# Reordering the last two attention rounds of an attention and mixture-of-experts kernel, and issuing each round's last weighted sum one slot later

## The reference, cut to what matters

```python
x = layernorm(x + attn(x))
scores = sigmoid(x @ router.T)            # 16 experts in 4 groups
...                                       # best 2 groups by (score + bias), best 4 experts in them
routed = sum over the 4 of weight * down_e(silu(gate_e(x)) * up_e(x))
x = layernorm(x + routed + shared(x))     # shared: two experts that see every token
```

## Time and profile before

| | |
|---|---|
| median of 3 runs | 1218.46 us (1216.24 to 1221.86) |
| the profiled execution's own time | 1211.09 us |
| its span, first to last instruction | 1209.3 us |
| mean granted TensorE clock | 0.936 of full speed |

### The profile page before, as it was taken

One profiled execution on the slowest core, in us unless ns is written; L12 is line 12 of the kernel. 1 busy time (PEld: TensorE's weight loads), 2 busy tenths in 40 slices (PEclk: granted clock), 3 DMA queues, 4 the chain that ended last, 5 costly groups with the idle time before them and its releaser, 6 DMA issues.

```text
span 1209.3 us, 25555 instructions
## 1 busy us (share of the span) xinstructions
PE 999.3 (83%) x8693; PEld 585.4 (48%) x8693; DVE 854.5 (71%) x1907; ACT 627.6 (52%) x1449; POOL 495.0 (41%) x712
## 2 busy tenths in 40 slices
PE   7976999879887999998899778888998787956950
PEld 3533333334432455555565445454564456845740
DVE  6666888768885667779767886788677669765543
ACT  4413777667444565755456457554565563314430
POOL 7922121133138211321473743113626745673334
PEclk9987999999888899999999999999999999987985
DMA  5843267421113444233276743222565744877942
GB/s 177 272 136 110 61 208 262 149 59 46 49 56 111 88 98 91 63 71 76 88 163 131 159 119 93 57 67 82 133 145 133 216 115 135 197 180 180 251 155 74
DMA packets 221978, 152.85 MB, mean 126 GB/s; under 512 B 139936, under 2 KB 199072, under 8 KB 221856
## 3 DMA queue, kind: packets, MB, share of 16 engines
q1 hardware_dynamic: 207936, 114.50, 37.5%
q0 software_dynamic: 12288, 33.57, 9.1%
q10 hardware_dynamic: 1632, 3.15, 0.9%
HBM read 50.36 MB, written 73.40 MB: 102 GB/s over the span
## 4 chain that ended last, share of the span: by engine, by line
PE 47%; DVE 17%; POOL 14%; issue 8%; DMA 5%; ACT 4%; SPq 4%; DVEq 0%; POOLq 0%; ACTq 0%
PE bank L711 11%; PE bank L566 9%; PE bank L537 8%; PE bank L550 7%; POOL a_pool L1021 6%; DVE a_mx L1201 4%; POOL rows L1013 3%; PE bank L724 3%; DMA a_pool<-outs,e_slot 2%; POOL a_PT L971 2%; DVE e_R L1447 2%; PE bank L596 2%; ACT a_PT L1082 2%; SPq L799 2%; PE bank L540 1%
## 5 line engine op out<-in xcount | busy, mean ns | idle before, releaser
L1201 DVE TENSOR_REDUCE a_mx<-bank 128x1 f32<-128x512 f32 (+3 forms) x720 | 423.6, 619 | 196.7 <-PE bank L540 123.0
L1082 ACT ACTIVATE a_PT<-bank 128x512 f32<-128x512 f32 (+4 forms) x832 | 373.6, 497 | 219.5 <-PE bank L550 215.9
L550 PE MATMUL bank<-a_QS,a_KS 113*128 113x512 f16 (+4 forms) x832 | 275.1, 338 | 31.9 <-DVE a_mx L1201 25.1
L971 POOL TENSOR_SCALAR_AFFINE_SELECT a_PT<-a_PT 128x256 f32<-128x256 f32 (+1 forms) x288 | 111.9, 395 | 437.5 <-ACT a_PT L1082 436.9
L537 PE MATMUL bank<-a_KS,a_QS 112*128 112x512 f16 (+4 forms) x832 | 264.3, 339 | 25.1 <-DMA a_KS<-k_dram 12.7
L566 PE MATMUL bank<-a_PT,a_VG 128*17 128x512 f32 (+4 forms) x1664 | 185.9, 519 | 28.1 <-POOL a_PT L971 28.1
L1021 POOL DMA_INDIRECT a_pool<-outs,e_slot x128 | 124.7, 975 | 82.2 <-issue 33.7
L1013 POOL DMA_INDIRECT rows<-e_XR,e_slot x128 | 127.8, 999 | 66.5 <-issue 35.4
L537 PEld LDWEIGHTS bank<-a_KS,a_QS 112*128 112x128 f16 x832 | 81.2, 100 | 121.8 <-ACT a_PT L1082 48.5
L1147 ACT ACTIVATE e_tq<-bank 128x256 f32<-128x256 f32 x136 | 51.1, 383 | 154.4 <-PE bank L711 154.0
L550 PEld LDWEIGHTS bank<-a_QS,a_KS 113*128 113x128 f16 x832 | 82.4, 100 | 98.9 <-DVE a_mx L1201 41.7
(11 more groups left out here) (156 smaller groups left out, 1289.1 us busy)
## 6 DMA issues: line engine op xcount, KB each, us to landing
outs<-e_ys SPq DMA_DIRECT2D x104, 256.0 KB
rows<-a_pool SPq DMA_DIRECT2D x48, 256.0 KB, 3.2
q_dram<-p_qk SPq DMA_DIRECT2D x32, 128.0 KB, 2.6
k_dram<-p_qk SPq DMA_DIRECT2D x32, 128.0 KB, 2.5
v_dram<-p_vs SPq DMA_DIRECT2D x8, 512.0 KB, 4.5
a_QS<-q_dram SPq DMA_DIRECT2D x64, 64.0 KB
a_KS<-k_dram SPq DMA_DIRECT2D x64, 64.0 KB
a_VG<-v_dram SPq DMA_DIRECT2D x16, 256.0 KB, 4.6
```

The source lines that it names most:

```text
L550: pe.matmul(ps[:, 0:(qc + 1) * CH - q0], KS[p][0:MR + 1, kt // NT, h % 2, kt % NT * P:kt % NT * P + P], QS[p][0:MR + 1, qc, h, q0 - qc * C ...
L971: pool.affine_select(out=a, in_=a, compare_op=ALU.is_ge, fill=0.0, base=q0 - (kt * P - WIN), pattern=[[0, 2], [1, w]], channel_multiplier= ...
L1082: act.activation(PT[(G + i) % 2][:, h, 0:w], bank("ST", G, i, h)[:, 0:w], ACT.Exp)\
L1201: dve.tensor_reduce(mx[:, piece, t // NT, heads[0]:heads[0] + n, t % NT], bank("S", G, u)[:, 0:n * w].rearrange("p (h k) -> p h k", h=n), ...
```

## The change

`SEQ` is a new order of the slots: rounds 0 to 13 as before, then first half of 14, first half of 15, second half of 14, second half of 15. Everything that counted slots (semaphore values, the two buffers of exponentials) now goes by `SLOT_NO`, the place in `SEQ`, and by `HALF_NO`. PE issues `weighted` of the slot before in each slot, across the ends of rounds too, and only the very last one at once; `out_copy` of a second half stands one slot into the next round. `shares` replaces `share`: it is the same for rounds 0 to 13, and for the last two the maximum's units are spread so that round 15's are done before each of its halves begins. The planner gets the chunks' places from the places of `outT`.

What the new plan puts where: for round 15's first half `maxT` at 372 and its store at 374, with scoresT of slot 187 (h = 374) needing it; for its second half 397 and 399, for h = 400. The first load of group 2 is at 372, `load_rows` for its eleventh pair is at 398 and needs the `gu` at 399. The first four slots of round 14 have 5, 6, 4 and 4 units instead of 4, 3, 3 and 3, and the fifth none instead of 2. Chunk 6's chain: `ont` 392 and 393, `x1t` 404 and 406, `lg` 409, `place` 422 to 425, scatters 425 to 435. Chunk 7's: `ont` 419 and 420, `lg` 434, `pos` 441. The last `gu` of group 2 is at 446 (two shared `gu` of chunk 6 and one more of group 2 between `pos` and it), the scatters of group 4 from 445, the gathers of group 2 from 459, the last `combine` of group 2 at 483, the last `y` at 535. Two `y` move from before 416 to behind it, and behind 483 there are 20 `gu` and 24 `y` of routed pairs as there were behind 482 before, and two shared `gu` and one `ysh` besides.

```diff
@@ -43,6 +43,17 @@
 FIRST = 1 + max(i for i, (qc, kt, _) in enumerate(SLOTS) if qc == 0 or kt < CH // P)
 ATT = NR * NSL

+PHASES = [(G, tuple(range(NH2))) for G in range(NR - 2)] + [(G, (half,)) for half in range(NH2) for G in (NR - 2, NR - 1)]
+SEQ = [(G, i) for G, halves in PHASES for i, (qc, _, _) in enumerate(SLOTS) if qc in halves]
+SLOT_NO = {at: n for n, at in enumerate(SEQ)}
+HALF_NO = {at: n for n, at in enumerate((G, half) for G, halves in PHASES for half in halves)}
+MASKED_TO = [sum(i in MASKED for _, i in SEQ[:n]) for n in range(ATT)]
+
+
+def last_read(G, half):
+
+    return SLOT_NO[G, max(i for i, (qc, kt, _) in enumerate(SLOTS) if half in (qc, kt * P // CH))]
+
...
-def share(slot):
-
-    cols = [(qc + 1) * CH - q0 + FIXED for qc, _, q0 in SLOTS]
-    lo, hi = (NU * sum(cols[:n]) // sum(cols) for n in (slot, slot + 1))
-    return [((n - TAIL) % NU, n >= TAIL) for n in range(lo, hi)]
+def shares():
+
+
+
+
+    at, ends_ = {}, {}
+
+    def spread(units, slots):
+        cols = [(SLOTS[i][0] + 1) * CH - SLOTS[i][2] + FIXED for _, i in slots]
+        for n, slot_ in enumerate(slots):
+            lo, hi = (len(units) * sum(cols[:m]) // sum(cols) for m in (n, n + 1))
+            at[slot_] = at.get(slot_, []) + units[lo:hi]
+
+    for G in range(NR - 2):
+        spread([(G, u) for u in range(NU - TAIL, NU)] + [(G + 1, u) for u in range(NU - TAIL)],
+               [(G, i) for i in range(NSL)])
+        ends_[G, 1], ends_[G, FIRST - 1] = (G, 1), (G + 1, 0)
+    G = NR - 2
+    first, last = ([i for i, sl in enumerate(SLOTS) if sl[0] == qc] for qc in range(NH2))
+    spread([(G, u) for u in range(NU - TAIL, NU)] + [(G + 1, u) for u in range(SECOND)], [(G, i) for i in first[:-1]])
+    spread([(G + 1, u) for u in range(SECOND, NU)], [(G + 1, i) for i in first] + [(G, i) for i in last[:-2]])
+    ends_[G, 1], ends_[G, first[-2]], ends_[G, last[-3]] = (G, 1), (G + 1, 0), (G + 1, 1)
+    return at, ends_
+
+
+SHARES, MAX_ENDS = shares()
...
+    for slot_, (G, half) in MAX_ENDS.items():
+        at = 2 * SLOT_NO[slot_] + (2 if G == NR - 1 and not half else 1 if half and G < NR - 1 else 3)
+        pe[at] = ("maxT", G, half)
+        act[at + 1].append(("mT", G, half))
+        sp[at + 2].append(("put_max", G, half))
+    out_at = {}
     for G in range(NR):
-        s0 = 2 * NSL * G
-        for (g, half, at) in ((G, 1, s0 + 3), (G + 1, 0, s0 + 2 * FIRST + 1)):
-            if g < NR:
-                pe[at] = ("maxT", g, half)
-                act[at + 1].append(("mT", g, half))
-                sp[at + 2].append(("put_max", g, half))
-        for qc, at in ((0, s0 + 2 * (HALF[0] + 3) + 1), (1, s0 + 2 * NSL + 5 if G < NR - 1 else s0 + 2 * NSL + 1)):
+        for qc in range(NH2):
+            last_slot = SLOT_NO[G, HALF[qc]]
+            out_at[G, qc] = at = 2 * last_slot + (7 if last_slot < ATT - 1 else 3)
             pe[at] = ("outT", G, qc)
             dve[at + 1].append(("normal", G, qc))
         if G + 2 < NR:
-            sp[s0 + 2 * FIRST + 1].append(("stack", G + 2, 0))
-            sp[s0 + 2 * NSL].append(("stack", G + 2, 1))
+            for half in range(NH2):
+                sp[2 * last_read(G, half) + 3 - half].append(("stack", G + 2, half))
         if G + 1 < NR:
-            sp[s0 + 4].append(("load_v", G + 1))
+            sp[2 * SLOT_NO[G, 0] + 4].append(("load_v", G + 1))

     for n in range(NX):
         at = 2 * (n // 3 * NSL + 4 * (n % 3) + 1)
@@ -143,7 +177,7 @@
     for n in range(UNITS_B):

     def chain(c, o, gap):

@@ -172,13 +206,12 @@

     ready, routed = {}, {}
...
-            pool[e + 4 if not late else tail - 10].append(("add_bo", c))
-            ready[c], at = chain(c, e, 0 if c == NC - 2 else 1)
-        gap = 1 if late else 2
+            e = out_at[b * NG + NG - 1, c % NH2] + (2 if c % NH2 == 0 else 1)
+            sp[min(e - 1, tail - 14)].append(("load_res", c))
+            pool[min(e + 4, tail - 10)].append(("add_bo", c))
+            ready[c], at = chain(c, e, 1)
+        gap = 1 if g == NGR - 1 else 2
         for n in range(RPARTS):
             dve[at + 2 + gap * n].append(("route", g, n))
         q = put(("pos", g), at + gap * RPARTS + 2)
@@ -195,7 +228,7 @@
             c, tile = shared_place(g, n)
             wanted.append((ready[c] + tile * 5, g, n))
         lo = routed[g] + 5
-        hi = routed[g + 1] - 7 if g + 2 < NGR and g < B - 2 else tail if g == B - 2 else lo
...
         lo = routed[g] + 5
-        hi = routed[g + 1] - 7 if g + 2 < NGR and g < B - 2 else tail if g == B - 2 else lo
+        hi = max(lo, min(routed[g + 1] - 7, tail)) if g + 1 < NGR else lo
...
         at = max(last[g] + 6, w)
-        if g == B - 2:
-            at = max(at, routed[NGR - 1] + 1)
         for t in range(GROUPS[g][2]):
...
             def weighted(G, i):
                 p = G % 2
                 qc, kt, q0 = SLOTS[i]
-                if i == 0:
+                n = SLOT_NO[G, i]
+                if kt == 0:
                     on.wait_ge(v_loaded[p], G // 2 * 16 + 16)
-                if kt == 0:
-                    on.wait_ge(s["ot_done"], G * NH2 + qc)
+                    on.wait_ge(s["ot_done"], HALF_NO[G, qc])
                 if i in MASKED:
-                    on.wait_ge(s["masked"], (G * len(MASKED) + MASKED.index(i) + 1) * 2)
+                    on.wait_ge(s["masked"], MASKED_TO[n] * 2 + 2)
                 else:
-                    on.wait_ge(s["exp_done"], G * NST + (i + 1) * HG)
+                    on.wait_ge(s["exp_done"], (n + 1) * HG)
                 for h in range(HG):
                     mm = pe.matmul(otbank[32 * h:32 * h + HD + 1, q0 - qc * CH:CH], VG[p][:, kt, h:VW:HG],
-                                   PT[(p + i) % 2][:, h, 0:(qc + 1) * CH - q0], start=(kt == 0),
+                                   PT[n % 2][:, h, 0:(qc + 1) * CH - q0], start=(kt == 0),
                                    stop=(i in HALF), skip_group_check=True)
                 mm.then_inc(s["pv_done"], 1)

@@ -575,7 +604,7 @@
                   .then_inc(s["mT_ready"], 1)
...
             pe.wait_ge(f["consts"], 4)

-            for G in range(NR):
-                round_of[0] = G
-
-                def some_scores(units):
-                    for u, ahead in units:
-                        if not ahead:
-                            scores(G, u)
-                        elif G + 1 < NR:
-                            scores(G + 1, u)
-
-                for i in range(NSL):
-                    rest, h2 = share(i), 2 * (G * NSL + i)
-                    for h in range(HG):
-                        scoresT(G, i, h)
-                        some_scores(rest[h:h + 1] if h < HG - 1 else ())
-                        if h == 1:
-                            fill(h2)
-                    if i:
-                        weighted(G, i - 1)
-                    some_scores(rest[HG - 1:])
-                    if i == NSL - 1:
-                        weighted(G, i)
-                    fill(h2 + 1)
+            for n, (G, i) in enumerate(SEQ):
+                units, ring = SHARES.get((G, i), []), "s_first" if G < NG else "scores"
+                for h in range(HG):
+                    scoresT(G, i, h)
+                    for g, u in units[h:h + 1] if h < HG - 1 else ():
+                        scores(g, u, ring)
+                    if h == 1:
+                        fill(2 * n)
+                if n:
+                    weighted(*SEQ[n - 1])
+                for g, u in units[HG - 1:]:
+                    scores(g, u, ring)
+                if n == ATT - 1:
+                    weighted(G, i)
+                fill(2 * n + 1)
...
             def out_copy(G, qc):
-                on.wait_ge(s["pv_done"], G * NSL + HALF[qc] + 1)
-                on.wait_ge(s["ott_ready"], G * NH2 + qc)
+                on.wait_ge(s["pv_done"], SLOT_NO[G, HALF[qc]] + 1)
+                on.wait_ge(s["ott_ready"], HALF_NO[G, qc])
                 act.copy(OTs[:], otbank[:]).then_inc(s["ot_done"], 1)
...
-            for G in range(NR):
-                for i in range(NSL):
-                    h2 = 2 * (G * NSL + i)
-                    for h in range(HG):
-                        exp(G, i, h)
-                        if h == 1:
-                            fill(h2)
-                    if i == 0 and G:
-                        out_copy(G - 1, NH2 - 1)
-                    if i == HALF[0] + 1:
-                        out_copy(G, 0)
-                    fill(h2 + 1)
+            for n, (G, i) in enumerate(SEQ):
+                for h in range(HG):
+                    exp(G, i, h)
+                    if h == 1:
+                        fill(2 * n)
+                if n and SEQ[n - 1][1] in HALF:
+                    out_copy(SEQ[n - 1][0], SLOTS[SEQ[n - 1][1]][0])
+                fill(2 * n + 1)
             out_copy(NR - 1, NH2 - 1)
```

More of the change, by code:

```diff
@@ L144, in plan @@
         sp[2 * NSL + 8 + n].append(("fill_rows", n))
-    span, tail = 2 * NSL * NG, 2 * ATT
+    tail = 2 * ATT
```

(2 more changed lines are left out.)

67 lines of the change are left out of this document (29 added, 38 removed).

## The result

The changed kernel takes 1230.45 us (median of 8, 1225.93 to 1232.0), the kernel before 1217.99 beside it (8 runs): ratio 1.0112, interval 1.0088 to 1.0136. **Slower by 12.5 us**, where 1216.8 and a range of 1205 to 1228 were predicted. The profiled execution took 1231.6 us, span 1229.9, clock 0.924. Before's profiled execution was faster than all eight of these runs, so the two traces differ by 20.5 us and the medians by 12.5; what a part is worth I take from medians.

What follows compares the result with a forecast made beforehand. PE was taken to bound the kernel, busy for 999 of 1209 us. The parts, -8.5 + 8.8 - 2.0 = -1.7 us on the median of 1218.46, gave 1216.8 us, with an 8-in-10 range of 1205 to 1228.

Steps and rivals of the forecast that it cites:

- Part 1: Ends of rounds: issuing the last weighted sum one slot later removes PE's waits for POOL's mask, -8.5 us.
- Part 2: Rounds 14 and 15: added work, new waits for the maximum's store and slow clock, less some savings, +8.8 us.
- (a) to (c): Round 15: PE waits of 4.6 and 3.6 us for the maximum's stores, plus 3.0 us of slow clock.
- (a): First half of round 15: PE waits 4.6 us for the maximum's store, behind group 2's first row load.
- (c): PE's clock at half speed after each of round 15's two store waits: 3.0 us, bounds 0 and 4.
- (d): Rounds 14 and 15: 0.85, 2 and 1.5 us of waits go or are caught up; chunk 6's chain adds 1.5.
- Part 3: The tail behind attention: an earlier window, then longer work behind it, -2.0 us in sum.
- the window ends 5.9 us earlier: Tail, up to group 2's last combine: 2.5 us from moved waits and work, 3.4 from chunk 7's chain.
- The +3.9 behind the window: Tail, work behind group 2's last combine: longer by two shared gu and one ysh, 3.9 us.
- The sign of being wrong: Tail: the prediction counts as wrong if the tail moves by over 6 us.
- The rival for slower: SP's queue in round 15: longest loads and landings, 16.7 us standing, 4 slow clock; total +8.3, 1226.8 us; chance 0.20.

Runs made afterwards that it cites:

- order_only: The changed kernel with the last weighted sum of rounds 0 to 13 issued at once again, as before the change: 1239.57 us, ratio 1.0187.
- mended: The changed kernel with round 15's maximum stores first, chunk 6's chain at its old places, and chunk 7's bias add behind the last slot: ratio 0.9984.
- late_sum_only: The kernel before with only the last weighted sum of rounds 0 to 14 issued in the next round's first slot: 1210.67 us, ratio 0.9945.
- chunk6_late: The changed kernel with chunk 6's chain and group 3's routing put back to their old places: 1224.96 us, ratio 1.0063.
- store_and_chunk6: The changed kernel with round 15's maximum stores ahead of the row loads and chunk 6's chain at its old places: 1219.58 us, ratio 1.0024.
- shared_early: The changed kernel with round 15's maximum stores first and the last two shared gu and last ysh back before group 2's combine: 1223.08 us, ratio 1.0042.

## Why the prediction was wrong

**Part 1 was right.** -8.5 us predicted, -7.7 measured by itself; the profile pair shows -6.4 by slot 182. The mask's list fell by 11.7 us; of that, 3.6 us went into waits for the store in rounds 2 and 3 (6.4 us in three waits against 2.8 in two; 2.5 in two in order_only, where those sums are issued at once). I had not looked at SP there, although the change brings each round's first scores nearer to its store.

**Part 2, (a) to (c), were right in place and near in size.** Waits of 2.9 and 4.2 us for 4.6 and 3.6, half clock behind both. I had set (a) between rows of the trace before and left part 1 out of both its sides. The load went out 4.7 us earlier than there (883.1 and not 887.8), since POOL gained from part 1 too, against "POOL gets no earlier"; PE came 3.3 us earlier (883.5 and not 886.85). That and a slightly quicker landing make 2.9 of 4.6. Taken away, the two waits gave 7.9 us in the medians and 9.2 in the traces, where I had 11.2 for (a) to (c). Of the 9.2, 4.5 are PE's busy time at the higher clock, over the 3.0 of (c) and its bound of 4: the slow clock lasted longer than one short stretch behind each wait. The rule of the Trainium skill (TensorE: Matmul & The Clock Gate, Terms), throttled time times one half, gives an estimate of some 7 us for what went (0.90 of 138.6 us against 0.95 of 129.4). The traces show 4.5, since in part of the throttled time PE had nothing to do.

**The step that failed is (d).** I let 0.85 us of round 14's end and 2 us of mask waits vanish, 1.5 be caught up, and put 1.5 us on chunk 6's chain: -2.85 in all. The traces have rounds 14 and 15 at +20.5, of which the two stands explain 9.2; that leaves 11.3, where I had 0.45 of work and (d), -2.4. Chunk 6's chain makes PE wait 6.4 us in the changed kernel (2.20, 2.23 and 1.98) for the 1.5 that I gave it, and the waits for a mask fell by 1.3 us and not by 2.85. In the medians the chain at its old place gave 5.5 us, 2 to 3 of them beyond the stands, and with the add out of the way 4 to 7. Group 1's last `y` had moved by two steps, and so had its gathers: two of them now stand behind the adds on POOL and in front of a mask. I had counted which slots meet gathers, but not what else was in POOL's queue at the same h. Of the reordering's 1.67%, the stores are 0.70; chunk 6's chain and the add together are up to 0.58, and 0.3 to 0.4 (4 to 5 us, the gap from mended to the late sums alone) stay unexplained. My bounds did not hold it (+18.3 against 20.5 in the traces), since (d) had no bounds of its own; the lower one was wrong as a sum too, -2.4 by its terms and not +0.

**Part 3 had the wrong sign.** -2.0 predicted, +6.4 in the traces (late_sum_only's tail is 3.0 longer than the one before as well, so that much may lie in the trace before, or in the late sums). The step: "the window ends 5.9 us earlier". It started as late as before, 50.8 us behind attention, and its last `combine` ended 1.0 us earlier, 124.9 us behind attention and not 125.9. I had taken chunk 6's waits and work out of the stretch, and the waits came back at chunk 7's `x1t` (7.09 us). I take it that the chain of chunk 7 sets its length; but with chunk 6's chain back in it the stretch is 52.7 and 54.0 us (chunk6_late, store_and_chunk6), so it was not quite free there either. The +3.9 behind the window was +8.2: 68.2 against 60.0 us, and 67.6 to 69.3 in the three other kernels with the same work there. With the shared work in its old place it is 64.1 to 65.7; but shared_early shows that putting it back wins nothing as a whole. The sign of being wrong that I had set here, a tail moved by over 6 us, was met.

The rival for slower had the right place, SP's queue, and ended at 1226.8; it had 0.20. It asked for the longest load and landing. The truth was medians there, and other causes elsewhere.

## What to carry to other kernels

When a chain of small steps is moved between other work, price each of its hand-overs: three of them cost 6.4 us of waits here, where one had been counted at 1.5. When a plan is shifted by even two steps, list for each engine what else its queue holds at those steps. Do not subtract waits from a stretch before you know what sets its length: 4.65 us of them went here, and the stretch stayed at 50.8. And the place of a store in SP's queue had no one rule: ahead of the loads it won 8 us in round 15, and lost 26 when it was done in every round.

## What the hardware showed that I had not expected

Two executions of one kernel placed a single wait at 7.6 and at 1.5 us (for the division on DVE, in slot 203), and a profiled one was the slowest of 12 (1217.5 with a median of 1210.7): a pair of traces was off by 8 us here. The slow clock outlasted the waits beside it: it stood at 0.50 from 940.5 to 957.6 us, and with the two waits for the store gone, PE did the same 1048 products in 4.5 us less. And in two groups of runs the kernel before took 1284 and 1285 us, 5% more than in the others, with the ratio between kernels the same: the late sums alone 0.9945 in the others and 0.9954 in these. Their traces show the excess in the tail (264 us against 228 for the same kernel) more than in attention.
